# 16-head attention on one core: ACT copies the turned probabilities of batch n-1 ahead of the exponentials of batch n

## The reference, cut to what matters

```
q = _rmsnorm(_rope(x @ wq.T), q_norm_w)      # 16 heads of 64
k = _rmsnorm(_rope(kv[..., :64]), k_norm_w)  # one head
scores = einsum('bqgtd,bqgsd->bqgts', q, k) / 8
attn = softmax(where(mask, scores, -1e30))
out = einsum('bqgts,bqgsd->bqgtd', attn, v)
return out @ wo.T
```

## Time and profile before

| | us |
|---|---|
| median of 3 runs | 3763.65 (3759.89 to 3793.61) |
| the profiled execution: time | 3754.26 |
| the profiled execution: span of its instructions | 3752.5 |
| around the span | 1.8 |
| busy in the span: PE / DVE / ACT / POOL | 3295.6 / 1916.6 / 1831.3 / 1024.6 |
| mean granted clock of TensorE | 0.947 of full speed |

### The profile page before, as it was taken

The page is one execution under the profiler, slowest core; times in us unless marked ns, Lnnn a source line. Parts: engine busy times, 40 slices in busy tenths (PEclk is TensorE's granted clock), DMA queues, the critical chain, the costliest instruction groups (busy, mean ns, idle before and its releaser), DMA issues. The chain is left out here.

```text
span 3752.5 us, 63158 instructions
## 1 busy us (share of the span) xinstructions
PE 3295.6 (88%) x23883; PEld 2083.9 (56%) x23883; DVE 1916.6 (51%) x3778; ACT 1831.3 (49%) x4130; POOL 1024.6 (27%) x950
## 2 busy tenths in 40 slices
PE   7999998798989888878988959997688888886998
PEld 6888886544646555525755633334455555553443
DVE  4555553402534344334947734445788888854111
ACT  1222224466465656545653523335466666653665
POOL 0000001001132222203726602222566666630000
PEclk9999998899999999978989969998899999997999
DMA  1000000000000000000000013220000000000000
GB/s 67 11 14 14 12 3 17 11 1 5 4 3 3 4 3 4 3 3 6 2 8 1 2 35 67 56 50 15 17 5 4 4 5 4 4 19 1 1 1 23
DMA packets 39780, 47.89 MB, mean 13 GB/s; under 512 B 8966, under 2 KB 36968, under 8 KB 38888
## 3 DMA queue, kind: packets, MB, share of 16 engines
q1 hardware_dynamic: 39480, 43.86, 4.5%
HBM read 38.14 MB, written 2.38 MB: 11 GB/s over the span
## 5 line engine op out<-in xcount | busy, mean ns | idle before, releaser
L452 ACT ACTIVATE p_hidden<-p_hid_ps,net_bias 128x344 f32<-128x344 f32 x816 | 382.6, 547 | 229.6 <-PE p_hid_ps L408 174.9
L425 PE MATMUL p_y_ps<-p_hidden,net_down 128*64 128x344 f32 x1632 | 280.8, 467 | 0.0
L2574 PE MATMUL p_c_ps<-p_ready,p_c1w 128*128 128x248 f32 (+5 forms) x960 | 244.0, 411 | 26.0 <-DVE p_ready L2732 26.0
L402 PE MATMUL p_hid_ps<-xn,net_up 64*128 64x344 f32 x1248 | 251.8, 484 | 16.0 <-PEq L2215 13.2
L2574 PEld LDWEIGHTS p_c_ps<-p_ready,p_c1w 128*128 128x128 f32 x960 | 179.7, 190 | 81.7 <-issue 26.6
L210 POOL TENSOR_SCALAR lin_hn<-lin_hn,columns 128x344 f32<-128x344 f32 x96 | 109.3, 1143 | 421.0 <-DVE lin_hn L199 420.8
L2413 DVE TENSOR_TENSOR p_hid<-p_silu,p_pair_ps 128x344 f32<-128x344 f32 x288 | 134.8, 509 | 173.4 <-PE p_pair_ps L2363 95.1
L1579 POOL TENSOR_TENSOR p_rot<-p_rot,p_cross 128x512 f32<-128x512 f32 x128 | 160.1, 1273 | 215.2 <-DVE p_cross L1716 215.2
L2395 ACT ACTIVATE p_silu<-p_pair_ps 128x344 f32<-128x344 f32 x288 | 116.0, 455 | 200.8 <-PE p_pair_ps L2352 200.8
L1592 POOL TENSOR_TENSOR p_prob<-p_prob,p_total 128x1024 f32<-128x1024 f32 (+1 forms) x128 | 185.3, 1469 | 15.2 <-DVE p_total L1742 15.2
L154 PE MATMUL p_var_ps<-p_square,average 128*128 128x344 f32 x432 | 171.9, 486 | 16.6 <-ACT p_square L172 16.5
(11 more groups left out here) (415 smaller groups left out, 7950.8 us busy)
## 6 DMA issues: line engine op xcount, KB each, us to landing
p_row<-gated_rows SPq DMA_DIRECT2D x192, 86.0 KB, 2.9
p_x<-in_tok_x SPq DMA_DIRECT2D x32, 192.0 KB, 2.3
out<-h SPq DMA_DIRECT2D x1, 2064.0 KB, 6.3
p_swapped<-xn SPq DMA_DIRECT2D x64, 32.0 KB, 1.9
p_c3w<-in_tok_c3w SPq DMA_DIRECT2D x1, 1280.0 KB, 9.2
thirds_fold<-in_L_fold SPq DMA_DIRECT2D x1, 1156.5 KB, 5.1
gated_w<-in_L2m_w SPq DMA_DIRECT2D x2, 512.0 KB, 4.0
p_val_high<-shared_values SPq DMA_DIRECT2D x1, 1024.0 KB, 6.8
```

The lines of the kernel that those rows point to most:

```text
L402: mm = pe.matmul(hid_ps[k % ring][:, 0:TILE], w_up[half(g), n, :], x[half(g), cols(t)], start=True, stop=not experts)
L425: mm = pe.matmul(y_ps[u][half(g), 0:TILE], w_down[:, n, :], hid[k % hidden_ring][:], start=n == 0, stop=last and not experts)
L452: act.activation(hid[k % hidden_ring][:], hid_ps[k % ring][:, 0:TILE], func, bias=b_up[:, n:n + 1]).then_inc(act_done.sem, 1)
L2574: mm = pe.matmul(to[:, :, j0:j1, w0:w1], weights(kh * reach + kw), src[:, :, j0 + kh - 2:j1 + kh - 2, w0 + kw - side:w1 + kw - side], star ...
```

## The change

It changes the order of one ACT queue. In a step, the two copies of the late rounds move ahead of the late exponential, and the copy of the early round ahead of the early exponential. No instruction is added or removed, no wait is changed, and nothing moves on another engine.

```diff
                     if n + 1 < BATCHES:
                         copy_queries(n + 1, 1)
-                    if n < BATCHES:
-                        exponentials(n, LATE)
                     if n >= 1:
                         copy_late(n - 1, 0)
                         copy_late(n - 1, 1)
                     if n < BATCHES:
+                        exponentials(n, LATE)
+                    if n >= 1:
+                        copy_early(n - 1)
+                    if n < BATCHES:
                         exponentials(n, EARLY)
                     if n >= 1:
-                        copy_early(n - 1)
                         copy_out(n - 1, LATE)
```

## The result

| | before | after |
|---|---|---|
| median of 16 runs, us | 3790.01 | 3726.28 |
| lowest to highest | 3754.75 to 3794.8 | 3714.27 to 3810.62 |
| profiled execution: span | 3752.5 | 3712.5 |
| stage: start of ACT's table load to start of the last tail matmul (line 1569) | 2638.7 to 3348.7: 710.0 | 2639.6 to 3312.0: 672.4 |
| first to last score of the loop (start of line 1441) | 2659.9 to 3326.2: 666.3 | 2660.8 to 3290.1: 629.3 |

A forecast was written before the change was run, and what follows sets the result against it. PE was taken to bound the stage, waiting for two ACT copies out of PSUM. 62 steps x 0.66 = 40.9 us, off 3754.26, gave 3713.4 for an execution like the profiled one; from about 3761 it gave 3720, range 3711 to 3737.

The forecast's parts named there:

- The bound: PE sets the stage's pace, waiting only for two ACT copies: 48.9 us at line 1482, 29.1 at line 1474.
- What stands in its place: Ahead of `mix_late` on PE, a new wait of about 0.25 us replaces the 0.77 ahead of early.
- The list of signs: What the later profile should show, including ACT idle 0.3 to 0.4 us ahead of the second late copy.
- the working: Step of 3020.33 worked out: late0's copy ends at 3027.38, late1's runs 3027.65 to 3028.26, `mix_late` starts at 3028.31.
- The term of the step, 0.66: `mix_late` on PE starts at 3028.31 against 3028.97, saving 0.66 us in each step.
- 62 steps: Steps of the stage counted as gaining, 62 x 0.66 = 40.9 us; the first one or two give little.
- The covers: Four checks in the short step, on exponentials, `copy_out`, DVE and POOL, each expected to cost nothing.
- the POOL wait: POOL's late scaling delays late0 by 0.35 us every second step, absorbed by the query-copy stall with 0.16 to spare.
- their room of 0.58: The late exponential on ACT ends at 3029.20, 0.58 us ahead of its DVE sum at 3029.78.
- the gain there is about half: Near the stage's end, without projection, PE waits for POOL in one step and gains about half.
- The slower rival: A loop through ACT's exponentials, 17.4 us against PE's 19.7 per two steps; 3793 us if 4.7 longer; chance 0.04.
- the base: Starting time of about 3761 us, from four executions at 3754.26, 3759.89, 3763.65 and 3793.61.

The follow-up runs named there:

- the POOL order alone: On the changed kernel, POOL scales batch n ahead of the norm of n+3 instead of behind it; loop 627.5 us against 629.3.
- the kernel with all copies first: The changed kernel with the early copy also ahead of both exponentials, behind the late copies; loop 630.4 us against 629.3.
- the exponentials pushed back by 1.8 us: The changed kernel with the early copy and the mixed values' copy also ahead of both exponentials; loop 644.6 us against 629.3.
- two edits that each win little: On the changed kernel: POOL scaling before norm (loop 627.5 us); second turned-query half before second early mix and its copy (622.3); both 608.8, against 629.3.

## Why the prediction was right, and where it was wrong

- **The bound** (PE waits only for two copies): right. The wait at line 1482 went, the 0.50 at line 1474 stayed in the short steps, and the largest wait of each of the other engines shrank with the step.
- **What stands in its place** (a wait of about 0.25 ahead of the mix): right, 0.24 in the short steps, and ACT idles 0.26 ahead of the second late copy. The list of signs had 0.3 to 0.4 for that; the working's own times, 3027.38 to 3027.65, give 0.27.
- **The term of the step, 0.66: too large, it is 0.62.** The working put 0.05 between the end of late1's copy and the mix; it is 0.10 (3009.25 to 3009.35), after 0.03 on the way to ACT. Those are the 8.99 and 10.74 that were worked out, against 9.03 and 10.78.
- **62 steps: nearly.** The first two give 0.00, the two behind them 0.58, the others 0.62 or 0.63 each, but for the last but one, which loses 0.36, about where half a gain was expected. That makes 37.0 in the loop, and 37.6 in the whole stage, instead of 40.9. The span fell by 40.0, but 0.9 was lost ahead of the stage and 3.3 won behind it, in stages whose code is the same. There the granted clock was at 0.50 for 314.0 us against 307.2 ahead of the stage, and for 56.0 against 64.3 behind it.
- **The covers.** DVE's idle time in short steps was used up and made good in the long ones; the POOL wait appeared (26 times, 0.25 in the step shown, 0.35 was worked out) and was absorbed by the wait for the query copy behind it (its copy ends at 3016.93, late1 starts at 3016.99), which the POOL order alone confirmed by winning nothing in the body; the exponentials had their room of 0.58, which the kernel with all copies first used without loss.
- **The step that got longer** is POOL's, and its sign was wrong in the prediction ("the gain there is about half"). In the last step but one there is no projection and no rotation left, so PE reaches the late round 0.8 us earlier in the step, and nothing absorbs the wait for POOL's scaling. PE at that place, before and then after:

```profile
3311.59 1.06 PE L1474 MATMUL p_t_ps<-ident,p_prob 128*128 128x128 f32 x8 [0.55 <-POOL p_prob L1592]
3276.39 1.06 PE L1474 MATMUL p_t_ps<-ident,p_prob 128*128 128x128 f32 x8 [1.16 <-POOL p_prob L1592]
```

  The scaling did not move up with PE: it starts 3.27 us after the step's first score before the change (3306.28 to 3309.55) and 3.89 after it (3270.46 to 3274.35). So this step pays back the 0.62 that the step before it had won, less the 0.26 by which the wait at line 1482 is still shorter. With POOL's order changed it took 9.60, 0.99 less than after.
- **The slower rival** (the loop through the exponentials) shows in the same step, but PE did not pay for it. The late copies wait for the late transposes, and the exponentials stand behind them. ACT and DVE in order of time, changed kernel:

```profile
3277.05 1.08 ACT L1646 ACTIVATE p_prob_t<-p_t_ps 128x512 f32<-128x512 f32 x2 [1.20 <-PE p_t_ps L1474]
3278.02 1.06 ACT L1640 ACTIVATE p_prob<-p_prob 128x1024 f32<-128x1024 f32 x1
```

```profile
3274.08 1.23 DVE L1732 TENSOR_TENSOR p_prob<-p_late_ps,p_stat 128x1024 f32<-128x1024 f32 x1
...
3275.93 0.69 DVE L1732 TENSOR_TENSOR p_prob<-p_early_ps,p_stat 128x512 f32<-128x512 f32 x1
3279.18 1.81 DVE L1740 TENSOR_REDUCE p_total<-p_prob 128x8 f32<-128x1024 f32 x2 [2.56 <-ACT p_prob L1640]
```

  DVE waits 2.56 us for the exponential, and yet the next step is 0.63 shorter than before. In the body of the loop even the exponentials pushed back by 1.8 us didn't make the kernel slower than before. The Trainium skill ("TensorE: Matmul & The Clock Gate", section "Architectural detail: the array is 16× 32×32, not 1× 128×128") states that "ACT/DVE are strict FIFO". The trace agrees: what the late exponential reads was there when its subtraction ended at 3275.31, and it starts at 3278.02, behind the copies, for which ACT had idled 1.20.
- **The step that failed is the base**: "From about 3761 I come to 3720", with 6 us for the base's scatter in the range. Of the four times known, 3793.61 got no weight. It was the other of two levels: 9 of before's 16 runs lie there and its median is 3790.01, 29 above the base that was used. The saving was forecast within 4 us (40.9 against 37.0). That the median after, 3726.28, is near the 3720 all the same is in part luck: 12 of its 16 runs fell in the lower group, at a median of 3723.8, against 3758.0 - 37.0 = 3721.0; had they split like before's, nine of them in the upper group, it would have come out at 3750 or more.

## What to carry to other kernels

When an engine waits for a copy, look at what stands in front of that copy in its engine's queue: what is read late can go behind what is waited for, as far as its reader's own schedule leaves room, and that room can be read off the two rows. A small wait can hide a second one, so two edits that each win little (1.8 and 7.0) can win 20 together. Compare step by step rather than by the total: an effect of 0.3 us a step is plain there, and what is left over can be placed. And of a base with one time 30 us above the rest, ask for its granted clock before calling it an outlier.

## What the runs showed of the hardware

- A stage whose code is the same in all these kernels stayed at the lower clock level (0.50, 1.2 GHz) for 92.2 us in one execution, with PE busy for 40.00 of 40 us in 1680 to 1720, and rose to the upper level after 20.5 us in twelve others (PE busy 37.27 of the same 40 in the one shown). The stage's matmuls took 81.5 us against 48.0, a difference nearly as large as this change.
- A fall of the clock to 0.50 for 3.4 us inside the loop cost 1.1 us in its step (11.70 against 10.59); otherwise the steps of two executions agreed within 0.01.
- From the end of an ACT copy to the PE instruction that waits for it took 0.05 us where PE waited with a transpose and 0.10 ahead of the mix; from PE's modelled end to ACT 0.03.
- A DVE maximum that starts right behind the reciprocal takes 1.16, and 1.22 to 1.23 after a wait; DVE's busy time over the span fell by 8.1 us (1916.6 to 1908.5) with the waits.
